# A fused attention and mixture-of-experts block: heads 0 to 7 joined inside the head loop, experts loaded later, token-major expert rows, and part of the last sum on TensorE

## The reference

```python
h = _layernorm(x) * (1 + ca) + sa
x = x + ga * attention(h)        # 16 heads of 16 columns, ALiBi bias, softmax over 1024 keys
h = _layernorm(x) * (1 + cb) + sb
logits = h @ router_w.T + expert_bias            # 16 experts
top_w, top_idx = top_k(softmax(logits), 4); top_w /= sum(top_w)
g, u = h @ gate_proj[e], h @ up_proj[e]          # 256 -> 224
out[e] = (silu(g) * u) @ down_proj[e]            # 224 -> 256
x = x + gb * sum_j top_w[j] * out[top_idx[j]]
```

## Time and profile before

| | |
|---|---|
| median of 3 runs | 493.79 us (493.55 to 493.92) |
| profiled execution: its own time, its span | 489.35 us, 487.5 us |
| mean granted TensorE clock | 0.903 of full speed |
| busy: PE, DVE, ACT, POOL | 401.6, 284.8, 237.0, 289.4 us |
| chain that ended last | PE 50%, DVE 15%, DMA 13%, issue 8%, SP's queue 6%, ACT 5% |

### The profile page before, as it was taken

How to read it: one execution, slowest core, us unless ns; L and a number is a source line. 1 busy time by engine, 2 the same in 40 slices (tenths; PEclk the granted TensorE clock), 3 DMA queues, 4 the chain that set the end, 5 groups by cost and what they waited for, 6 DMA issues and landing times.

```text
span 487.5 us, 10785 instructions
## 1 busy us (share of the span) xinstructions
PE 401.6 (82%) x3712; PEld 218.0 (45%) x3714; DVE 284.8 (58%) x646; ACT 237.0 (49%) x503; POOL 289.4 (59%) x291
## 2 busy tenths in 40 slices
PE   4898749999999999999876627799899997999700
PEld 1764214344444444444435514366565554656400
DVE  3951948888998998999313784233333333333256
ACT  1273826777777777777870330233333333333211
POOL 5657617778889877777266001466566566665422
PEclk9598959999999999999995855899999999999955
DMA  7624735776333566658569900222222222232074
GB/s 217 257 39 153 239 117 137 176 190 203 109 106 105 155 170 168 170 159 239 165 151 298 279 5 2 73 77 73 64 84 66 75 67 66 75 76 56 0 273 157
DMA packets 38184, 64.50 MB, mean 132 GB/s; under 512 B 8177, under 2 KB 20903, under 8 KB 38014
## 3 DMA queue, kind: packets, MB, share of 16 engines
q1 hardware_dynamic: 25198, 34.95, 22.7%
q0 software_dynamic: 11584, 26.89, 21.6%
q10 hardware_dynamic: 1360, 2.10, 1.3%
HBM read 47.78 MB, written 18.01 MB: 135 GB/s over the span
## 4 chain that ended last, share of the span: by engine, by line
PE 50%; DVE 15%; DMA 13%; issue 8%; SPq 6%; ACT 5%; another core or an unknown queue 1%; POOL 0%; DVEq 0%; POOLq 0%; ACTq 0%
PE ps L1618 13%; PE ps L1460 7%; PE ps L1628 7%; PE ps L1479 7%; PE ps L1443 4%; ACT probs L703 3%; DVE x_sb L1290 3%; PE ps L1609 3%; DMA al_rows<-w_gu 3%; DVE junk L1096 3%; DMA x_sb<-in_x 2%; PE ps L1602 2%; DMA hT<-inv_rows 2%; PE ps L1465 2%; SPq L517 2%
## 5 line engine op out<-in xcount | busy, mean ns | idle before, releaser
L1096 DVE CUSTOM_DVE_ANT_0 junk<-ps,bias_t 128x1024 bf16<-128x1024 f32 x128 | 155.3, 1219 | 32.6 <-PE ps L1443 31.4
L703 ACT ACTIVATE probs<-ps 128x512 f32<-128x512 f32 x256 | 137.1, 603 | 47.5 <-DVE ps L1107 39.6
L1460 PE MATMUL ps<-q_st,k_st 122*32 122x512 bf16 x1024 | 84.5, 390 | 7.1 <-DMA q_st<-m_row 4.5
L1618 PE MATMUL ps<-w_gu,probs 128*128 x188 | 81.8, 558 | 0.0
L972 POOL DMA_INDIRECT probs<-xn_rows,bias_t x47 | 48.0, 1020 | 53.4 <-DVE bias_t L1259 38.6
L979 POOL DMA_INDIRECT z_rows<-probs,bias_t x47 | 48.1, 1023 | 49.9 <-DVE probs L1282 33.2
L1479 PE MATMUL ps<-probs,v_st 128*32 128x256 f32 x1024 | 66.7, 380 | 0.7 <-ACT probs L703 0.7
L797 POOL TENSOR_SCALAR bias_t<-dist,slopes 128x1920 f32<-128x1920 f32 x13 | 66.5, 5112 | 0.0
L1275 DVE TENSOR_TENSOR probs<-probs,ps 128x224 f32<-128x224 f32 x47 | 18.2, 387 | 81.5 <-ACT probs L765 56.6
L1443 PE MATMUL ps<-kx,qx 64*128 64x512 bf16 x256 | 44.2, 393 | 9.2 <-DMA kx<-k_rows 4.7
L754 ACT ACTIVATE probs<-ps,modc 128x128 f32<-128x128 f32 x47 | 21.5, 457 | 61.1 <-PE ps L1602 40.0
(11 more groups left out here) (202 smaller groups left out, 486.1 us busy)
## 6 DMA issues: line engine op xcount, KB each, us to landing
k_st<-k_rows SPq DMA_DIRECT2D x32, 192.0 KB, 5.0
qx<-q_rows SPq DMA_DIRECT2D x32, 128.0 KB, 2.6
w_gu<-in_gate_proj POOLq DMA_DIRECT2D x16, 224.0 KB, 4.2
w_gu<-in_up_proj POOLq DMA_DIRECT2D x16, 224.0 KB, 5.1
w_dn<-in_down_proj POOLq DMA_DIRECT2D x16, 224.0 KB, 6.4
q_st<-q_rows SPq DMA_DIRECT2D x16, 192.0 KB, 3.7
kx<-k_rows SPq DMA_DIRECT2D x32, 64.0 KB, 2.7
os_rows<-o_sb SPq DMA_DIRECT2D x14, 128.0 KB
```

What stands on the lines that cost most here:

```text
L703: act.activation(probs[:, j % 4, CH * ch:CH * ch + CH], ps_st[(NU * c + u) % 3], ACT.Exp).then_inc(exp_done, 1)
L1096: dve.tensor_tensor_reduce(junk[:, n % 2, :], ps_max[n % 2].rearrange("p b n -> p (b n)"), bias_t[:, g % 2, off:off + T], 1.0, -3.0e38, AL ...
L1460: last = pe.matmul(ps_st[n % 3][32 * g:32 * g + 32, :], k_st[0:R_ALL, ch, s, r:r + 32], q_st[0:R_ALL, s, CH * ch:CH * ch + CH], start=True ...
L1618: last = pe.matmul(ps[:, 2 + c % 2, 0:2 * INTER], xT[:, c % 2, kk, :], w_gu[:, bass.ds(e, 1), kk, :].rearrange("p x n -> p (x n)"), start= ...
```

## The change

1. The join is in two parts. Heads 0 to 7: sums and heads 0 to 3 in step 9, heads 4 to 7 in step 10, inversion by DVE at the end of step 10, store in step 11, loads of the inverses in steps 12 and 13, multiplication in step 15. Heads 8 to 13 keep their place in step 14, and are multiplied behind head 15 (`normalise_last`).
2. Experts 0 to 4 are loaded in steps 7, 8, 10, 12 and 13; the other 11 once all six loads of the join have landed.
3. `merge_o` of head 15 stands ahead of the first three `project_o`; the eight turns are transposes.
4. `xn_rows` and `z_rows` are kept by token (row p*8+t, and (p*8+t)*4+j): a partition's rows are adjacent in HBM.
5. 18 `keep_warm` matmuls ahead of the 32 table matmuls, 36 behind the last expert tile.
6. Tiles 0, 2, 3, 5 and 7 are summed by PE: ACT makes 20 diagonal matrices of the weights during routing, PE multiplies them with `z_sb` and adds in PSUM, DVE adds the residual. DVE sums tiles 1, 4 and 6. POOL and ACT sum none. SP and ACT issue four loads each.

```diff
+LOAD_STEPS = (7, 8, 10, 12, 13)
+WARM_TABLE = 18
+WARM_TAIL = 36
-SUM_DVE = (0, 1, 3, 4, 6, 7)
-SUM_POOL = (2, 5)
+SUM_DVE = (1, 4, 6)
+SUM_PE = tuple(t for t in range(NT) if t not in SUM_DVE)
...
+        def load_rows(eng, t):
+            eng.dma_start(z_sb[t], z_rows.rearrange("(p t j) e -> p t j e", t=NT, j=TOPK)[:, t]).then_inc(z_in[t], 16)
...
-                sp.dma_start(z_sb[t], z_rows.rearrange("(j t p) e -> p t j e", p=P, j=TOPK)[:, t]).then_inc(z_in[t], 16)
+            for t in range(0, NT, 2):
+                load_rows(sp, t)
...
+            act.wait_ge(w_top_done, 1)
+            for n, t in enumerate(SUM_PE):
+                for j in range(TOPK):
+                    act.activation(diags[TOPK * n + j], ident[:], ACT.Identity, scale=top_w[:, t, j:j + 1]).then_inc(diag_done, 1)
             call_table(ACT.Silu)
...
+                if c == P // D + 1:
+                    join_sums(0)
+                    join_heads(0, 0, 4)
+                if c == P // D + 2:
+                    join_heads(0, 4, 8)
+                if c == P // D + 3:
+                    store_inverses(0)
+                if c == P // D + 4:
+                    load_inverses(0, 0, 4)
+                if c == P // D + 5:
+                    load_inverses(0, 4, 8)
                 if c == H - 2:
-                    join_heads()
+                    join_sums(1)
+                    join_heads(1, 0, H_LOOP - P // D)
+                    store_inverses(1)
+                    load_inverses(1, 0, H_LOOP - P // D)
...
             steps(step)
-            load_expert(H - 1)
+            pool.wait_ge(att_in, 16 * 6)
+            for n in range(len(LOAD_STEPS), NX):
+                load_expert(n)
...
+                    if c == H - 1 and p == 1:
+                        dve.wait_ge(att_in, 16 * 4)
+                        normalise(slice(0, P), 0)
...
             normalise_last(H - 1)
+            dve.wait_ge(att_in, 16 * 6)
+            normalise(slice(0, P - 2 * D), 1)
             dve.wait_ge(turned, 2)
...
             sum_pv(H - 1, 3)
+            merge_o(H - 1)
             pe.wait_ge(wo_done, 1)
             pe.wait_ge(att_done, 1)
             for t in range(3):
                 project_o(t, 0)
-            merge_o(H - 1)
             pe.wait_ge(att_last, 2)
...
-                last = pe.matmul(ps_turn[t // TC][:, t % TC * P:t % TC * P + P], attn_l[:, b, g, :], ident[:],
-                                 start=True, stop=True)
+                last = pe.transpose(ps_turn[t // TC][:, t % TC * P:t % TC * P + P], attn_l[:, b, g, :], ident[:])
...
             last.then_inc(before_ready, 1)
+            keep_warm(WARM_TABLE, 6)
...
             tiles(pe, tile, -1, MAX_TILES + 2)
+            keep_warm(WARM_TAIL, 4)
+            pe.wait_ge(diag_done, TOPK * len(SUM_PE))
+            for n, t in enumerate(SUM_PE):
+                pe.wait_ge(z_in[t], 16)
+                if n >= 4:
+                    pe.wait_ge(acc_done, SUM_PE[n - 4] + 1)
+                for j in range(TOPK):
+                    last = pe.matmul(ps[:, n % 4, 0:E], diags[TOPK * n + j], z_sb[t][:, j, :], start=(j == 0),
+                                     stop=(j == TOPK - 1))
+                last.then_inc(sum_ready, 1)
```

More of the change, by code:

```diff
@@ L263, in adaln_block @@
         hi_rep = q_st[:].rearrange("p s n -> p (s n)")[:, 0:(NTAB + 1) * tab_n]
+        diags = [attT[:, k, n * P:n * P + P] for k in range(KE) for n in range(NT)]
+        diags += [dist[:, n * P:n * P + P] for n in range(W_DIST // P)]
         z_sb = [k_st[:, s].rearrange("p s n -> p (s n)").bitcast(F32) for s in range(NCH)]
@@ L277, in adaln_block @@
         ps_ot = ps[:, 0, 0:2 * G * (D + 1)].rearrange("p (b g d) -> p b g d", b=2, g=G)
-        ps_turn = [ps[P - 2 * D:P, 4 + n, :] for n in range(2)]
+        ps_turn = [ps[0:2 * D, 4 + n, :] for n in range(2)]
         y1_banks = (1, 2, 3, 0)
@@ L589, in _ @@
                 sp.wait_ge(scattered[s], 16 * len(range(s, MAX_TILES, 4)))
+            for t in range(0, NT, 2):
+                load_rows(sp, t)
             for t in range(NT):
-                sp.dma_start(z_sb[t], z_rows.rearrange("(j t p) e -> p t j e", p=P, j=TOPK)[:, t]).then_inc(z_in[t], 16)
[L592 to L596, removed]
+                sp.wait_ge(acc_done, t + 1)
                 sp.dma_start(out[P * t:P * t + P, :], x_sb[:, t, :]).then_inc(out_stored, 16)
@@ L767, in _ @@
             tiles(act, tile, -1, MAX_TILES + 1)
[L770 to L775, removed]
+            for s in range(4):
+                act.wait_ge(scattered[s], 16 * len(range(s, MAX_TILES, 4)))
+            for t in range(1, NT, 2):
+                load_rows(act, t)
         @block.gpsimd
@@ L904, in load_expert, with join_sums, join_heads, store_inverses @@
                                a["down_proj"][n:n + 1].rearrange("x (k p) n -> p x k n", p=IH)).then_inc(w_done, 16)
-            def join_heads():
+            parts = ((0, P // D), (P // D, H_LOOP))
+            def join_sums(k):
+                first, last = parts[k]
                 for s in range(2):
[L909 to L919, removed]
+                    pool.wait_ge(o_stored[s], 16 * last // 2)
+                pool.dma_start(sum_c[NT * first:NT * last, :],
+                               os_rows[first:last, D, :].rearrange("h (a n) -> h a n", n=P)).then_inc(sums_in, 16)
+            def join_heads(k, a, b):
+                pool.dma_start(attT[D * a:D * b, k, :], os_rows[parts[k][0] + a:parts[k][0] + b, 0:D, :]).then_inc(att_in, 16)
+            def store_inverses(k):
+                first, last = parts[k]
+                pool.wait_ge(sums_done, k + 1)
+                pool.dma_start(inv_rows[first:last].rearrange("h (a n) -> (h a) n", n=P),
+                               sum_c[NT * first:NT * last, :]).then_inc(inv_stored, 16)
+            def load_inverses(k, a, b):
+                pool.wait_ge(inv_stored, 16 * k + 16)
+                first = parts[k][0]
+                pool.dma_start(inv[D * a:D * b, k, :],
+                               inv_rows[first + a:first + b].unsqueeze(1).broadcast_to([b - a, D, T])).then_inc(att_in, 16)
             def step(c):
@@ L1284, in _ @@
             tiles(dve, tile, -1, MAX_TILES + 2)
-            for t in SUM_DVE:
-                dve.wait_ge(z_in[t], 16)
-                for j in range(TOPK):
-                    ins = dve.scalar_tensor_tensor(out=x_sb[:, t, :], in0=z_sb[t][:, j, :], scalar=top_w[:, t, j:j + 1],
-                                                   in1=x_sb[:, t, :], op0=ALU.mult, op1=ALU.add)
-                    if j < TOPK - 1:
-                        link(ins)
+            for t in range(NT):
+                if t in SUM_DVE:
+                    dve.wait_ge(z_in[t], 16)
+                    for j in range(TOPK):
+                        ins = dve.scalar_tensor_tensor(out=x_sb[:, t, :], in0=z_sb[t][:, j, :], scalar=top_w[:, t, j:j + 1],
+                                                       in1=x_sb[:, t, :], op0=ALU.mult, op1=ALU.add)
+                        if j < TOPK - 1:
+                            link(ins)
+                else:
+                    n = SUM_PE.index(t)
+                    dve.wait_ge(sum_ready, n + 1)
+                    ins = dve.tensor_tensor(x_sb[:, t, :], ps[:, n % 4, 0:E], x_sb[:, t, :], ALU.add)
                 ins.then_inc(acc_done, 1)
```

41 lines of the change are left out of this document (17 added, 24 removed).

## The result

| | before | after |
|---|---|---|
| median of 20 runs each, same chip | 494.24 us (489.33 to 500.38) | 491.66 us (484.63 to 496.95) |
| ratio to before | | 0.9894, 95% interval 0.9857 to 0.9930 |
| span of the profiled execution | 487.5 us | 484.3 us |
| busy PE, DVE, ACT | 401.6, 284.8, 237.0 us | 423.5, 279.9, 239.2 us |
| mean granted clock | 0.903 | 0.936 |

The change makes the kernel 5.2 us faster (3.5 to 7.1); 12.3 us were forecast, and a median of 481.5 us. Some executions of either kernel fall into a slower state, and the ratio leaves them out, which is why it is lower than the quotient of the two medians. On a second chip, 12 runs against 17 of before gave 0.9897 (0.9858 to 0.9936): the ratio is repeated.

What follows compares the result with a forecast made beforehand. PE was taken to bound the attention loop, with waits on transfers at its end. Join -8.1, routing -1.5 and tail -2.7 gave -12.3 us, from 493.79 to 481.5 us; range 477.5 to 487.5.

Steps and rivals of the forecast that it cites:

- The join: Loop's end, last product with V to first residual: 8.6 us less; 8.1 us less after the loop's price.
- The inversion behind step 10: Attention loop: one more inversion on DVE, costing between 0 and 0.96 us, taken as 0.5.
- The loop: Attention loop, steps 9 to 13: two to three more POOL transfers a step cost nothing, POOL being busy 8.22 of 11.40 us.
- The table: Routing: warm matmuls let part of the 32 table matmuls run at full clock, 1.5 us less, bounds 0 and 2.9.
- The bound of 0: Routing: lower bound of the gain from warm matmuls; at half clock the table matmuls gain nothing.
- its rival: Routing: warm matmuls give nothing, as the clock falls back or factor loads bind; 483.0 us, chance 10%.
- The tail: After the experts: DVE's last sum ends at 480.6 instead of 483.33 us, 2.7 us less.
- The stores behind it stay: Kernel's end: the stores after the last sums are unchanged, so no gain was counted there.
- D: Before the experts: weights land late at 165 GB/s and PE waits, 15.6 us late, 497.1 us; chance 5%.
- C: Tail: rows 32 KB apart slow the result loads to 210 GB/s, 8.8 us later, 490.3 us; chance 5%.
- A: Tail: PE's sums run at half clock, 3.5 us a tile, 487.8 us in all; chance 13%.

Runs made afterwards that it cites:

- the probe: Kernel issuing only the join's transfers with 2 KB loads beside them, without attention or experts; four heads landed after 6.2 us in one transfer, 3.7 us as four.

## Why the prediction was wrong

- **The join: right.** 8.6 us forecast at the loop's end; 8.6 to 9.1 from the two profiles of before, with clock 1.00 from 264.5 to 269 us. The inversion behind step 10 was put at 0.5 and costs 0.56.
- **The loop: the step that failed.** The prediction said "POOL issues two to three transfers more in steps 9 to 13 and is busy 8.22 of 11.40 us" and put them at nothing: of its 8.1 us for the join, only 0.5 is a price of the loop. That is a reason why POOL has time for them, not why the transfers are free of effect on others. Step 13 lasts 15.1 to 19.0 us in the seven profiles that keep its transfers as they are, three of the change (16.03, 18.22, 17.94) and four of kernels that differ elsewhere (15.10, 17.00, 18.29, 19.01): a mean stall of 6.0 us. Taken away in two ways, it gives 4.5 and 6.7 us back. The wait is for the 2 KB `m_row` load, beside a 256 KB transfer that keeps 4 of 16 DMA engines busy in the probe. Why the stall varies between 3.7 and 7.6 us stays open. What I left out was to go through each moved transfer, ask which load of another queue goes out at that moment, and how much delay that one bears.
- **The table: a second step that failed, sized at 1.5, is 0.** The table matmuls were taken to run faster at full clock; they take 5.84 us there against 5.83 at half. The bound of 0 and its rival ("the factor loads of the table matmuls bind and not the clock", 483.0) had been named; the latter is close, only that it is the reading of the moving operand. The stretch from residual to gate product is no shorter (39.2 to 40.6 us against 39.2 to 39.8, on average 0.6 longer, which is within the spread).
- **The tail: sized at 2.7, is 4.6.** The end of DVE's sums moved by 2.3 us behind PE's last expert product in the first pair of profiles (22.31 to 20.02) and by 3.1 in the second (23.13 to 20.01): as forecast, with tiles of 1.9 to 2.0 us that wait for their loads. The rest I had put at nothing ("The stores behind it stay"): from DVE's last sum to the span's end 4.2 us became 2.3, in every profile with the changed tail 2.1 to 2.4. I did not test why, so this gain of 1.9 us is luck, and it hides a part of the miss.
- **Weights, layout of the results, half clock in the tail** (rivals D, C and A): none happened. The last weights were issued at 285.73 and PE did not wait; rows 32 KB apart were read at 415 GB/s; the tail's clock was 1.00, and without the warm matmuls one tile of five ran slow.

With the measured sizes, as means over the profiles of the table, the sum is -8.8 (join) + 0.6 (step 10) + 6.0 (step 13) + 0.3 (step 14, 10.54 instead of 10.25 us) + 0.6 (residual to gate) - 4.6 (tail) = -5.9 us, within the interval of the timed -5.2 us. The start, up to the first copy, is not in it: it was 0.5 to 4.8 us later in the changed kernel's profiles, and two profiles of before cannot tell that from chance. The expert phase, from first gate to last product, was 153.7 us in both first profiles; elsewhere it lay between 140 and 158 us and went more with the chip than with the kernel, so nothing shows that it takes part in the difference.

## What to carry to other kernels

A transfer that is moved under other work is not free because its issuing engine has time: list what other queues issue in the same microseconds, above all the small loads that something waits for, and how late each may land. Keep large transfers wide in their slowest dimension, even at the price of more issues: here 22 more issues cost nothing. Before paying for a higher clock, check that the instruction's time differs between the two levels at all.

## What the runs showed of the hardware

- 2, 4 and 8 blocks of 64 KB in one transfer landed after 5.2, 6.2 and 6.0 us, at DMA shares of 0.12, 0.24 and 0.51; one block after 2.4 us, four transfers of one block after 3.7 us in all.
- A matmul with 96 moving columns read at a stride of 64 bytes took 0.18 us at either clock, and 0.087 us with them contiguous at clock 0.50.
- A DVE product of 128 x 1024 bf16 values took 0.68 us written contiguously and 4.70 us written at a stride of 256 bytes.
- Loads with 4 KB runs 32 KB apart: 415 GB/s at a share of 1.02; the runs of before gave 375 GB/s.
- Chips differ in one phase: between 330 and 430 us, in the experts, PE was busy 93.5 us in the changed kernel on the first chip and 99.8 in the same kernel on the second, both at clock 1.00. The cause stays open.
